# Layers 5 and 6, tokens, the state space and the gate scores of an audio tower, taken batch by batch into the groups of the convolution stream, whose loop is written out

## The chip, the cores and the metric

The kernel runs on 1 core of one Trainium2 chip. The metric is the device time of one execution, in microseconds (us). A core has five engines that each work through a queue of their own in program order: TensorE (PE in the rows; PEld is its weight load), VectorE (DVE), ScalarE (ACT), GpSimd (POOL) and SyncE (SP, which here only starts transfers). They wait for each other through semaphores. TensorE writes its products to PSUM, eight banks of 128 x 512 float32.

## The reference, cut to what matters

Eight rows of 120,000 samples pass seven strided convolutions, each followed by a layer norm over the 128 channels and a gelu. What comes out, 374 tokens of 128 channels per batch, is normed, projected to 192 features and taken through a diagonal state-space layer, a mixture of four experts, a two-way scan and a soft mixture of 64 experts.

```python
CONVS = [(128, 10, 5)] + [(128, 3, 2)] * 4 + [(128, 2, 2)] * 2
h = x[:, None, :]
for w, g, b, s in zip(conv_ws, ln_gs, ln_bs, strides):
    h = gelu(layernorm(conv1d(h, w, s)), exact)          # norm over the channels
h = layernorm(swapaxes(h, 1, 2)) @ proj_w + proj_b       # tokens
h = h + state_space(norm(h))   # x_s = A_bar x_(s-1) + B_bar u_s;  y_s = Re(C x_s) + D u_s
h = h + experts4(norm(h))      # scores = norm(h) @ gate_w + gate_b, argmax over 4
h = h + two_way_scan(norm(h))
h = h + soft_mixture(norm(h))  # 64 experts of 16 slots
```

## The kernel before

**setup** loads and centres the convolution weights. On DVE it also runs `ssm_tables` (L808 on, with helpers at L819 to L821), the decay and the tables of cosines and sines of the state space, for which ACT gives exponentials and sines in `ssm_functions` (L795 on). SP loads all small weights of later stages. A block of code ends when all engines have ended it.

**stream** computes layers 0 to 4 of all batches as one long sequence of 47 chunks (`CHUNKS`), in a hardware loop (`Fori`) on each engine. A chunk has eight groups (`GROUPS`), each the work of one half of a layer: on PE `conv(j, g)` makes 12 float32 products of 128x128 (6 for layer 4) at L255; ACT squares them (L312); DVE sums (`stats`, L352, and L355); POOL takes the power -0.5 (`root`, L426); DVE multiplies (`normalise`, L363); PE turns the result back to channels (`transposes`, L264), two groups late (`LAG = 2`); ACT applies the gelu (L330). Layer 0 of the next chunk, its patches and its windows are put between the groups: on PE behind groups 0 to 7 (L276, L286, L292, L302), on DVE in `copy_windows` (group 0), `patch_squares` and `patch_stats` (1), `copy_patches` (2, 3) and `split_patches` (6, 7), on POOL in `patch_root` (2 to 5). The order is written out by hand. Four PSUM banks take the products in turn (`BANKS = 4`). Behind the loop three last groups (`TAIL`) drain layers 3 and 4 one after the other. Layer 4 of all batches stays in the tile `l4`.

After the stream four stages each handle all eight batches before the next stage begins:

- **layers56** (L622 products, L641 squares, L659 and L663 sums, L675 roots, L654 multiplication, L614 turn, L634 gelu): layer 5 in 16 groups, layer 6 in 8, with a group's turn two groups late.
- **tokens**: turn, norm, turn back, affine, projection (L742), into the tile `h`.
- **state_space**: norm, turn, the products with B (L903, L904: 374 columns each), rotation by the tables (L969), two scans (L978, L979), rotation, the products with C (L916, L917), addition to `h` (L960). Batch b + 1 is prepared while b is computed; four banks take input products and turned tiles.
- **gate**: SP starts the loads of small tables, the clearing of a buffer of 2.6 MB in HBM (`sorted`), and the loads of the soft mixture's weights (`phA`, `phB`, `b2s`); DVE norms all 24 tiles; PE turns them and makes the scores (L1056 to L1067); DVE picks the expert and the row of each token. The block ends when the row numbers are there and SP has seen its loads land.

Behind it come `routed_ffn` and the later stages, the same in both kernels.

Of the kernel before, what the change touches and what calls it, by code (L numbers as in the profile page):

```python
# [12 lines left out]
P = 128  # L13
# [37 lines left out]
BANKS = 4  # L51
# [35 lines left out]

def setup(nc, T, S, io):

    with nc.Block() as block:  # L90
        @block.sync
        def _(sp):
# [11 lines left out]
            for name in ("proj_w", "BTa", "gate_wa", "Wia", "Wca", "Wcb", "Woa", "Wob", "lncol"):  # L104
                sp.dma_start(T[name][:], io[name]).then_inc(S["small_loaded"], 16)
            for name, rows in (("BTb", HIGH), ("gate_wb", HIGH), ("Wib", HIGH), ("Wcc", HIGH)):
                sp.dma_start(T[name][rows], io[name]).then_inc(S["small_loaded"], 16)
            sp.dma_start(T["mcol"][:, 0:15], io["mcol"]).then_inc(S["small_loaded"], 16)
            for name, n in (("rows", 3 * D), ("gate_row", 2 * N_EXPERT)):
                src = bass.AP(io[name].tensor, 0, [[0, TOK], [1, n]])  # L110
                sp.dma_start(view(T[name][:], [[1, n]]), src).then_inc(S["rows_loaded"], 16)
            sp.wait_ge(S["cols_loaded"], 16)
            sp.wait_ge(S["small_loaded"], 16 * 14)
            sp.wait_ge(S["rows_loaded"], 16 * 2)

        @block.gpsimd
        def _(pool):
# [8 lines left out]
            for name, rows in (("BTb", LOW), ("gate_wb", LOW), ("Wib", LOW), ("Wcc", LOW), ("phB", LOW)):  # L126
                pool.memset(T[name][rows], 0.0)
# [6 lines left out]
        def _(dve):  # L134
# [24 lines left out]
            dve.wait_ge(S["readout_loaded"], 16)  # L159
            ssm_tables(dve, T, S)  # L160

# [18 lines left out]
        @block.scalar  # L180
        def _(act):
            act.wait_ge(S["ident_ready"], 1)
            act.activation(T["identb"][:, :], T["ident"][:, :], ACT.Copy).then_inc(S["identb_ready"], 1)
            ssm_functions(act, T, S)
# [15 lines left out]
def stream(nc, T, S, io):  # L200
# [16 lines left out]
    def event(j, g):  # L217

        return GROUPS[g] + (g % BANKS, g % 2, count(j, g), P * j)

# [93 lines left out]
    def gelu(act, e, carry=None):  # L314
# [11 lines left out]
        if layer == 4:  # L326
            dst = T["l4"][:, :, bass.ds(column, P)]
# [106 lines left out]

    with nc.Block() as block:
        @block.sync
        def _(sp):
# [5 lines left out]
            with sp.Fori(0, CHUNKS) as j:  # L443
                load(j + 3)
            sp.wait_ge(S["x_loaded"], 16 * (CHUNKS + 3))

        @block.tensor
        def _(pe):
# [8 lines left out]
            with pe.Fori(0, CHUNKS) as j:  # L457
                for g in range(NG):
# [11 lines left out]
                    layer0s(pe, j + 1, L0_END.get(g, ()))  # L470
            transposes(pe, event(CHUNKS - 1, 6))
            transposes(pe, event(CHUNKS - 1, 7))
            for n, e in enumerate(TAIL):
                pe.wait_ge(S["h_ready"], END + n)
                products(pe, e)
                transposes(pe, e)

        @block.scalar
        def _(act):
            for i in range(8):  # L480
                gelu0(act, 0, i)
            with act.Fori(0, CHUNKS) as j:
                for g in range(NG):
# [8 lines left out]
                    for i in L0_END.get(g, ()):  # L492
                        gelu0(act, j + 1, i)
            gelu(act, event(CHUNKS - 1, 6))
            gelu(act, event(CHUNKS - 1, 7), CHUNKS + 1)
            for e in TAIL:
                square(act, e)
                gelu(act, e, CHUNKS + 1)

        @block.vector  # L500
        def _(dve):

            for name, n in (("normed", NG), ("turned", NG - LAG), ("h_ready", NG - LAG), ("summed", NG),
                            ("squared", NG), ("var_ready", NG), ("rstd_ready", NG), ("conv_done", NG), ("zz_done", 1)):
                dve.sem_inc(S[name], n)
            for c in range(2):
# [8 lines left out]
            with dve.Fori(0, CHUNKS) as j:  # L515
# [17 lines left out]
            for e in TAIL:  # L533
                stats(dve, e)
                normalise(dve, e)

        @block.gpsimd
        def _(pool):
# [3 lines left out]
            with pool.Fori(0, CHUNKS) as j:  # L542
# [4 lines left out]
            for e in TAIL:  # L547
                root(pool, e)

# [3 lines left out]


D = 192
D1, D2 = 128, D - 128
LOW, HIGH = slice(0, D2), slice(D2, P)
LEN = 374
TOK = 125
TPB = 3  # L560
SEQ = TOK * TPB
TILES = B * TPB
N_EXPERT, HID = 4, 768
HC = HID // P

ROUTED = (B * SEQ + N_EXPERT * (P - 1)) // P
SOFT_E, SLOT, SOFT_H = 64, 16, 384
SLOTS = SOFT_E * SLOT
SC = SLOTS // P
SHC = SOFT_H // P  # L570


class Link:


    def __init__(self, eng, sem, per_round=0, round_=0):
        self.eng, self.sem, self.base, self.n = eng, sem, round_ * per_round, 0

    def __call__(self, ins):
        self.n += 1  # L580
        ins.then_inc(self.sem, 1)
        self.eng.wait_ge(self.sem, self.base + self.n)


L4_FIRST = 513


def layers56(nc, T, S):

    psY, psT = T["psY"], T["psT"]

    def five(g, t, k):
        at = (L4_FIRST + k) // 2 + g * SEQ + t * TOK
        return T["l4"][:, (L4_FIRST + k) % 2, at:at + TOK]

    def six(g, t, k):  # L600
        at = 2 * (g * SEQ + t * TOK) + k
        return T["l5"][:, at:at + 2 * TOK - 1:2]

    def run(layer, groups, src, dst):
        s = {k: S[f"{k}{layer}"] for k in ("conv", "sq", "sum", "var", "rstd", "norm", "turn", "out")}
        with nc.Block() as block:
            @block.tensor
            def _(pe):
                def turn(g):
                    pe.wait_ge(s["norm"], g + 1)  # L610
                    if g >= 1:
                        pe.wait_ge(s["out"], g)
                    for t in range(TPB):
                        mm = pe.transpose(psT[:, t * TOK:(t + 1) * TOK], T["yn"][0:TOK, g % 2, t * C:(t + 1) * C],  # L614
                                          T["ident"][0:TOK, 0:TOK])
                    mm.then_inc(s["turn"], 1)
                for g in range(groups):
                    if g >= BANKS:
                        pe.wait_ge(s["norm"], g - BANKS + 1)
                    for t in range(TPB):  # L620
                        for k in range(2):
                            mm = pe.matmul(psY[g % BANKS][0:TOK, t * C:(t + 1) * C], src(g, t, k),  # L622
                                           T["wt"][:, 12 + 2 * (layer - 5) + k, :], start=(k == 0), stop=(k == 1))
                    mm.then_inc(s["conv"], 1)
                    if g >= LAG:
                        turn(g - LAG)
                for g in range(groups - LAG, groups):
                    turn(g)

            @block.scalar  # L630
            def _(act):
                def gelu(g):
                    act.wait_ge(s["turn"], g + 1)
                    act.activation(T[dst][:, g * SEQ:(g + 1) * SEQ], psT[:, 0:SEQ], ACT.Gelu,  # L634
                                   bias=T["cols"][:, 8 + layer:9 + layer],
                                   scale=T["cols"][:, layer:layer + 1]).then_inc(s["out"], 1)
                for g in range(groups):
                    act.wait_ge(s["conv"], g + 1)
                    if g >= 2:
                        act.wait_ge(s["sum"], g - 1)  # L640
                    act.activation(T["sq"][0:TOK, g % 2, 0:TPB * C], psY[g % BANKS][0:TOK, 0:TPB * C], ACT.Square)\  # L641
                        .then_inc(s["sq"], 1)
                    if g >= LAG:
                        gelu(g - LAG)
                for g in range(groups - LAG, groups):
                    gelu(g)

            @block.vector
            def _(dve):
                def normalise(g):  # L650
                    dve.wait_ge(s["rstd"], g + 1)
                    if g >= 2:
                        dve.wait_ge(s["turn"], g - 1)
                    dve.tensor_tensor(T["yn"][0:TOK, g % 2, 0:TPB * C].rearrange("p (t c) -> p t c", c=C),  # L654
                                      psY[g % BANKS][0:TOK, 0:TPB * C].rearrange("p (t c) -> p t c", c=C),
                                      bcast(T["rstd"][0:TOK, g % 2, 0:TPB], C), ALU.mult).then_inc(s["norm"], 1)
                for g in range(groups):
                    dve.wait_ge(s["sq"], g + 1)
                    dve.reduce_sum(T["ss"][0:TOK, g % 2, 0:TPB],  # L659
                                   T["sq"][0:TOK, g % 2, 0:TPB * C].rearrange("p (t c) -> p t c", c=C), axis=AX.X)\  # L660
                        .then_inc(s["sum"], 1)
                    dve.wait_ge(s["sum"], g + 1)
                    dve.tensor_scalar(T["var"][0:TOK, g % 2, 0:TPB], T["ss"][0:TOK, g % 2, 0:TPB], 1.0 / C, EPS,  # L663
                                      ALU.mult, ALU.add).then_inc(s["var"], 1)
                    if g >= 1:
                        normalise(g - 1)
                normalise(groups - 1)

            @block.gpsimd
# [1627 lines left out]
```

## Time and profile before

| | |
|---|---|
| median of 3 runs | 2589.71 us (2587.6 to 2591.08) |
| the profiled execution: time | 2585.41 us |
| the profiled execution: span | 2583.6 us |
| busy share of the span | PE 87%, DVE 54%, ACT 44%, POOL 34% |
| granted TensorE clock, mean | 0.933 of full speed |

The span is the time from the first to the last recorded instruction; 1.8 us lie around it. Shares are averages over stages with different limits, so they don't say what a change in one stage is worth. In the rows a clock of 1.00 is 2.4 GHz and 0.50 is 1.2 GHz.

### The profile page before, as it was taken

The numbers are of one execution on the slowest core, as the hardware profiler recorded it, in microseconds if no ns is written. First come the engines' busy times: TensorE is split into PE (matmuls) and PEld (weight loads), VectorE is DVE, ScalarE is ACT, GpSimd is POOL, SyncE is SP. The second block draws the span as 40 slices with busy tenths as digits, with TensorE's granted clock in tenths as the row PEclk, the third lists the DMA queues.
The fourth block names the chain that finished last, engine by engine and source line by source line (L and its number), as shares of the span: only waits on it lengthen the run. The fifth ranks groups of instructions, "written<-read, shape, count | busy, mean of one in ns | idle before, by whom it ended". The sixth has DMA issues, their size and how long they took to land. (4 is left out here: it accounts for less than half of the span.)

```text
span 2583.6 us, 48262 instructions
## 1 busy us (share of the span) xinstructions
PE 2236.5 (87%) x16651; PEld 2045.1 (79%) x16651; DVE 1394.8 (54%) x3521; ACT 1132.4 (44%) x2178; POOL 869.8 (34%) x758
## 2 busy tenths in 40 slices
PE   0999999999999999999987555199698788877988
PEld 0899999999999999999987434199455566667988
DVE  6566665666656666666654686212376465552222
ACT  0556656565565665656554100033233444432320
POOL 3545555454554545545443222500231000000000
PEclk9999999999999999999998776599899799988999
DMA  1000000000000000000000003578000011017976
GB/s 55 4 4 3 4 3 3 4 3 4 3 3 3 3 4 3 4 3 3 4 3 1 1 0 69 154 222 230 23 15 9 25 42 42 37 48 235 327 232 215
DMA packets 78675, 132.08 MB, mean 51 GB/s; under 512 B 13924, under 2 KB 56590, under 8 KB 77836
## 3 DMA queue, kind: packets, MB, share of 16 engines
q1 hardware_dynamic: 55052, 101.61, 12.6%
q10 hardware_dynamic: 17984, 20.30, 2.4%
q0 software_dynamic: 5568, 9.27, 1.2%
q8 instruction: 39, 0.64, 0.1%
q14 instruction: 32, 0.26, 0.0%
HBM read 102.57 MB, written 28.49 MB: 51 GB/s over the span
## 5 line engine op out<-in xcount | busy, mean ns | idle before, releaser
L255 PE MATMUL banks<-t_wt,t_l 128*128 128x128 f32 x8508 | 1043.0, 276 | 4.1 <-ACT t_l L330 2.9
L255 PEld LDWEIGHTS banks<-t_wt,t_l 128*128 128x128 f32 x8508 | 1012.5, 193 | 18.1 <-ACT t_l L330 3.9
L426 POOL TENSOR_TENSOR t_rstd<-t_var,t_minus_half 128x4 f32<-128x4 f32 (+1 forms) x379 | 366.8, 968 | 626.4 <-DVE t_var L355 626.4
L363 DVE TENSOR_TENSOR t_yn<-banks,t_rstd 128x512 f32<-128x512 f32 (+1 forms) x379 | 249.2, 657 | 344.9 <-POOL t_rstd L426 326.5
L312 ACT ACTIVATE t_sq<-banks 128x512 f32<-128x512 f32 (+1 forms) x379 | 215.9, 570 | 480.2 <-PE banks L255 477.9
L432 POOL TENSOR_TENSOR t_zrstd<-t_zvar,t_minus_half 128x8 f32<-128x8 f32 x196 | 320.8, 1638 | 43.2 <-DVE t_zvar L390 43.2
L343 ACT ACTIVATE t_l<-banks,t_cols 128x512 f32<-128x512 f32 x384 | 292.7, 778 | 47.6 <-PE banks L302 41.9
L352 DVE TENSOR_REDUCE t_ss<-t_sq 128x4 f32<-128x512 f32 (+1 forms) x379 | 244.5, 645 | 110.9 <-ACT t_sq L312 110.9
L330 ACT ACTIVATE t_l<-banks,t_cols 128x512 f32<-128x512 f32 (+2 forms) x381 | 285.1, 748 | 10.7 <-PE banks L264 5.9
L264 PE MATMUL banks<-t_ident,t_yn 128*128 128x128 f32 x1426 | 219.4, 273 | 11.5 <-DVE t_yn L363 10.3
L264 PEld LDWEIGHTS banks<-t_ident,t_yn 128*128 128x128 f32 x1426 | 173.5, 141 | 25.4 <-DVE t_yn L363 11.3
L697 POOL TENSOR_TENSOR t_nrstd<-t_nvar,t_minus_half 125x3 f32<-125x3 f32 x40 | 34.5, 861 | 394.4 <-DVE t_nvar L691 394.4
L302 PE MATMUL banks<-t_p60T,t_w 120*128 120x512 bf16 x384 | 140.3, 386 | 1.1 <-ACT t_l L343 1.0
L1277 ACT ACTIVATE t_G<-banks,t_b1T 128x128 f32<-128x128 f32 x162 | 47.9, 365 | 87.1 <-PE banks L1244 87.0
L1673 ACT ACTIVATE t_EDT<-banks,t_ltm 128x374 f32<-128x374 f32 x64 | 36.8, 575 | 111.3 <-DVE t_ltm L1779 111.0
L1916 DVE TENSOR_SCALAR t_a<-t_H,t_egA 128x128 f32 x64 | 22.1, 346 | 115.3 <-PE banks L1849 107.6
L1848 PE MATMUL banks<-t_a,t_w 128*128 128x128 f32 x384 | 75.8, 279 | 5.6 <-DMA t_w1x<-in_w1x 5.6
L1979 PE MATMUL banks<-t_yb,t_ectb 128*125 128x192 f32 (+1 forms) x384 | 65.6, 333 | 14.4 <-DVE t_yb L1954 10.4
L1979 PEld LDWEIGHTS banks<-t_yb,t_ectb 128*125 128x125 f32 (+1 forms) x384 | 64.0, 192 | 16.0 <-DVE t_yb L1954 10.7
L1779 DVE TENSOR_REDUCE t_ltm<-banks 128x1 f32<-128x374 f32 x64 | 34.8, 544 | 75.8 <-PE banks L1563 75.8
L1849 PE MATMUL banks<-t_a,t_w1x 65*128 65x128 f32 x384 | 75.7, 279 | 0.0
L1856 PE MATMUL banks<-t_w,t_eg 128*128 128x192 f32 x384 | 73.6, 328 | 0.7 <-ACT t_eg L1875 0.6
(311 smaller groups left out, 3428.0 us busy)
## 6 DMA issues: line engine op xcount, KB each, us to landing
t_w<-in_w SPq DMA_DIRECT2D x64, 480.0 KB
t_w<-in_w SPq DMA_DIRECT2D x27, 576.0 KB, 6.5
ect<-t_ECT SPq DMA_DIRECT2D x16, 750.0 KB, 3.2
t_w1a<-in_w1a SPq DMA_DIRECT2D x27, 384.0 KB, 3.8
t_ectb<-ect ACTq DMA_DIRECT2D x5, 1500.0 KB, 7.9
t_w1x<-in_w1x SPq DMA_DIRECT2D x64, 97.5 KB
ys<-t_ye ACTq DMA_DIRECT2D x64, 96.0 KB
t_yb<-ys ACTq DMA_DIRECT2D x8, 768.0 KB, 11.0
```

Of the source, the lines that this page charges most:

```text
L255: mm = pe.matmul(psY[bank][:, t * C:(t + 1) * C], src[:, at:at + P], T["wt"][:, 3 * (layer - 1) + k, :], start=(k == 0), stop=(k == 2))
L264: mm = pe.transpose(psT[:, t * P:(t + 1) * P], T["yn"][:, par, t * C:(t + 1) * C], T["ident"][:, :])
L302: pe.matmul(psL[i % 2][:, :], T["w60"][:, slot, :], p60T[:, 4 * q:4 * q + 4, :].rearrange("r a p -> r (a p)"), start=True, stop=True).then ...
L312: act.activation(T["sq"][:, par, 0:n], psY[bank][:, 0:n], ACT.Square).then_inc(S["squared"], 1)
L330: act.activation(dst, psT[:, 0:n].rearrange("c (t p) -> c t p", p=P), ACT.Gelu, bias=T["cols"][:, 8 + layer:9 + layer], scale=T["cols"][:, ...
L343: act.activation(view(T["l0"][:, :], [[2 * BLOCK, 4], [1, P]], block_at(0, 8 * q + slot)), psL[i % 2][:, :].rearrange("c (a p) -> c a p", ...
L352: dve.reduce_sum(T["ss"][:, par, 0:n], T["sq"][:, par, 0:n * C].rearrange("p (t c) -> p t c", c=C), axis=AX.X)\
L363: dve.tensor_tensor(T["yn"][:, par, 0:n * C].rearrange("p (t c) -> p t c", c=C), psY[bank][:, 0:n * C].rearrange("p (t c) -> p t c", c=C), ...
L426: pool.tensor_tensor(T["rstd"][:, par, 0:n], T["var"][:, par, 0:n], T["minus_half"][:, 0:n], ALU.pow)\
L432: pool.tensor_tensor(T["zrstd"][:, s], T["zvar"][:, s], T["minus_half"][:, 0:POS // 4], ALU.pow)\
L1848: pe.matmul(o, T["w12"][:, r, c * P:(c + 1) * P], T["a1"][:, r % RING, :], start=True, stop=False)
L1979: mm = pe.matmul(pO[k % 2][0:n, 0:D], T["ectb"][:, b % MIX_RING, c, t * TOK:t * TOK + n], T["yb"][:, b % MIX_RING, c, :], start=(c == 0), ...
```

## The change

The stages layers56, tokens, state_space and the scores half of gate are gone. Their work is cut into 33 steps per batch (`CHAIN = 33`), and one step is put behind each group of the stream, on each engine's queue, once the batch's part of `l4` is there: batch b has the steps 0 to 32 behind the groups of chunk 8 + 6b and on. Batches 0 to 5 fit whole; of batch 6 the last three chunks take steps 0 to 23, the three groups of `TAIL` steps 24 to 26, and steps 27 to 32 and all 33 of batch 7 come behind `TAIL`. All steps share one bank, `psQ`, so each waits for the one before. The stream has `BANKS = 3`. `ssm_tables` becomes a generator whose 40 pieces are put behind DVE's first 40 groups, `ssm_function` stands at three places of ACT's stream, and SP's small loads move from setup behind the second load of the stream. The loops on all five engines are written out. `phA`, `phB` and `b2s` now share memory with the steps' tiles and are still loaded in gate.

```diff
-BANKS = 4
+BANKS = 3
...
+    def chain_at(j, g):
+
+        if j < FIRST_OF:
+            return 0, -1
+        return (j - FIRST_OF) // PERIOD, NG * ((j - FIRST_OF) % PERIOD) + g
...
+    def pe_conv56(pe, b, i):
+        e = 3 * b + i
+        if i == 0:
+            pe.wait_ge(S["h_ready"], last_column_of(b))
+            if b >= 1:
+                pe.wait_ge(S["z_read"], b)
+        else:
+            pe.wait_ge(S["q_out"], e)
+        for t in range(TPB):
+            for k in range(2):
+                src = five(b, i, t, k) if i < 2 else six(t, k)
+                mm = pe.matmul(psQ[0:TOK, t * C:(t + 1) * C], src, T["wt"][:, 12 + 2 * (i // 2) + k, :],
+                               start=(k == 0), stop=(k == 1))
+        mm.then_inc(S["q_conv"], 1)
+
+    def pe_turn56(pe, b, i):
+        pe.wait_ge(S["q_norm"], 3 * b + i + 1)
...
+    def pe_turn_u(pe, b, part):
+        if part == 0:
+            pe.wait_ge(S["u_ready"], b + 1)
...
+    def pe_state_outputs(pe, b, part):
+        if part == 0:
+            pe.wait_ge(S["x_ready"], b + 1)
...
+    def pe_chain(pe, b, step):
...
+        if step == 0:
+            pe_conv56(pe, b, 0)
+        if step == 2:
+            pe_turn56(pe, b, 0)
+        if step == 3:
+            pe_conv56(pe, b, 1)
+        if step == 5:
+            pe_turn56(pe, b, 1)
+        if step == 6:
+            pe_conv56(pe, b, 2)
+        if step == 8:
+            pe_turn56(pe, b, 2)
+        if step == 9:
+            pe_tokens(pe, b)
+        if step == 11:
+            pe_channels(pe, b)
+        if step == 12:
+            pe_project(pe, b, 0)
+        if step == 13:
+            pe_project(pe, b, 1)
+        if step == 16:
+            pe_turn_u(pe, b, 0)
+        if step == 17:
+            pe_turn_u(pe, b, 1)
+        if step == 18:
+            pe_state_inputs(pe, b, 0)
+        if step == 19:
+            pe_state_inputs(pe, b, 1)
+        if step == 26:
+            pe_state_outputs(pe, b, 0)
+        if step == 27:
+            pe_state_outputs(pe, b, 1)
+        if step == 30:
+            pe_turn_v(pe, b, 0)
+        if step == 31:
+            pe_turn_v(pe, b, 1)
+        if step == 32:
+            pe_scores(pe, b)
...
+    def dve_chain(dve, b, step):
+        if step == 0:
+            dve_stats56(dve, b, 0)
+        if step == 1:
+            dve_normalise56(dve, b, 0)
...
+        if step == 9:
+            dve_token_stats(dve, b)
+        if step == 10:
+            dve_token_norm(dve, b)
...
+        if step == 14:
+            dve_u_stats(dve, b)
+        if step == 15:
+            dve_u(dve, b)
+        if step == 18:
+            dve_rotate_inputs(dve, b, 0)
+        if step == 19:
+            dve_rotate_inputs(dve, b, 1)
+        if step == 20:
+            dve_join_inputs(dve, b)
+        if step == 21:
+            dve_scan(dve, 0)
+        if step == 22:
+            dve_scan(dve, 1)
+        if step == 23:
+            dve_rotate_states(dve, b, 0)
+        if step == 24:
+            dve_rotate_states(dve, b, 1)
+        if step == 25:
+            dve_rotate_states(dve, b, 2)
...
+        if step == 28:
+            dve_v_stats(dve, b)
+        if step == 29:
+            dve_v(dve, b)
...
-            with pe.Fori(0, CHUNKS) as j:
+            for j in range(CHUNKS):
                 for g in range(NG):
                     conv(pe, j, g)
...
                     layer0s(pe, j + 1, L0_END.get(g, ()))
+                    pe_chain(pe, *chain_at(j, g))
             transposes(pe, event(CHUNKS - 1, 6))
             transposes(pe, event(CHUNKS - 1, 7))
             for n, e in enumerate(TAIL):
                 pe.wait_ge(S["h_ready"], END + n)
                 products(pe, e)
                 transposes(pe, e)
+                pe_chain(pe, B - 2, LEFT + n)
+            for step in range(LEFT + len(TAIL), CHAIN):
+                pe_chain(pe, B - 2, step)
+            for step in range(CHAIN):
+                pe_chain(pe, B - 1, step)
...
                     if g == 7:
                         split_patches(dve, j + 2, 1)
+                    next(tables, None)
+                    dve_chain(dve, *chain_at(j, g))
...
         @block.gpsimd
         def _(pool):
+            pool.memset(T["phB"][LOW], 0.0)
             pool.memset(T["w1b"][LOW, :, :], 0.0).then_inc(S["zero_ready"], 1)
```

## Rows read from the trace of the kernel before

**Rows 1.** Busy time by stage: one stream chunk, TAIL, layers56, tokens, state_space, gate.
```profile
core 0: us, PE busy (x) PEld busy (x) DVE busy (x) ACT busy (x) POOL busy (x), PEclk, DMA share, GB/s
1179.30:1206.10 26.80, 26.80 (x242) 26.27 (x241) 16.47 (x38) 16.16 (x29) 14.10 (x13) 1.00 0.01 3
1337.00:1368.00 31.00, 14.62 (x67) 12.06 (x65) 7.21 (x20) 6.47 (x13) 3.41 (x4) 0.66 0.01 3
1368.00:1423.00 55.00, 46.94 (x358) 43.91 (x359) 28.72 (x72) 25.98 (x47) 20.41 (x24) 0.91 0.00 1
1423.00:1461.00 38.00, 23.19 (x99) 17.92 (x99) 23.54 (x104) 5.97 (x9) 6.80 (x8) 0.76 0.00 1
1461.00:1585.40 124.40, 71.04 (x208) 47.23 (x208) 104.65 (x217) 6.86 (x16) 29.24 (x24) 0.71 0.00 0
1585.40:1636.60 51.20, 31.00 (x148) 30.31 (x148) 23.22 (x111) 8.43 (x18) 10.20 (x9) 0.50 0.40 87
```

**Rows 2.** Timeline of setup: start, duration, engine, line, operation [idle before it].
```profile
17.18 0.16 DVE L823 TENSOR_TENSOR t_sv<-t_sv 128x1 f32<-128x1 f32 x1
17.28 12.16 SPq L102 DMA_DIRECT2D t_band<-t_gram  x16
...
17.60 1.28 ACT L804 ACT_TABLE_LOAD   x1
...
42.91 2.29 DVE L163 TENSOR_REDUCE t_wmean<-t_wt 128x16 f32<-128x2048 f32 x1
...
48.21 0.70 PE L286 MATMUL banks<-t_ident,t_xs 128*85 128x128 f32 x2 [31.15 <-PEq L90]
```

**Rows 3.** PE by line: the stream chunk of Rows 1, then one line of the whole run.
```profile
L255 PE MATMUL banks<-t_wt,t_l 128*128 128x128 f32 x180 | 21.9, 275 | 0.0
...
L1352 PE MATMUL banks<-t_xA,t_Wca 128*128 128x374 f32 x144 | 49.2, 477 | 0.0
```

**Rows 4.** Timeline of one stream chunk around the groups 0, 7 and again 0.
```profile
1181.93 0.67 DVE L352 TENSOR_REDUCE t_ss<-t_sq 128x4 f32<-128x512 f32 x1
...
1184.09 0.69 DVE L363 TENSOR_TENSOR t_yn<-banks,t_rstd 128x512 f32<-128x512 f32 x1 [1.29 <-POOL t_rstd L426]
...
1185.69 0.60 PE L264 MATMUL banks<-t_ident,t_yn 128*128 128x128 f32 x4
...
1206.18 2.84 PE L255 MATMUL banks<-t_wt,t_l 128*128 128x128 f32 x24
...
1207.58 0.23 DVE L416 COPY t_p<-t_p 128x320 bf16<-128x320 bf16 x1
```

**Rows 5.** Operations of the stages that move, by line, whole run: busy us, mean ns.
```profile
L697 POOL TENSOR_TENSOR t_nrstd<-t_nvar,t_minus_half 125x3 f32<-125x3 f32 x40 | 34.5, 861 | 394.4 <-DVE t_nvar L691 394.4
...
L969 DVE TENSOR_TENSOR t_seq<-t_seq 128x374 f32<-128x374 f32 x32 | 17.9, 560 | 1.8
...
L978 DVE TENSOR_TENSOR_SCAN t_seq<-t_sv,t_seq 128x374 f32<-128x374 f32 x8 | 7.5, 937 | 0.3
```

**Rows 6.** Timeline: the last group of TAIL, its products and its gelu.
```profile
1359.99 2.93 PE L255 MATMUL banks<-t_wt,t_l 128*128 128x128 f32 x12 [1.10 <-ACT t_l L330]
...
1366.02 0.56 ACT L330 ACTIVATE t_l<-banks,t_cols 128x256 f32<-128x256 f32 x1 [2.67 <-PE banks L264]
```

**Rows 7.** PE's timeline between layer 5 and layer 6, and the clock there.
```profile
1402.92 6.95 PE L622 MATMUL banks<-t_wt,t_l 128*125 128x128 f32 x36 [1.01 <-PEq L606]
...
1404.00:1406.00 2.00, 2.00 (x11) 2.00 (x11) 0.00 (x0) 0.14 (x1) 0.00 (x0) 0.50 0.02 4
```

**Rows 8.** Gate: its first memset, and the DMA share where its loads end.
```profile
1585.44 3.93 POOL L1038 MEMSET t_w1b<- 64x4608 f32 x1 [21.15 <-POOLq L891]
...
1608.00:1610.00 2.00, 2.00 (x11) 2.00 (x11) 0.00 (x0) 0.00 (x0) 0.00 (x0) 0.50 0.33 41
1610.00:1612.00 2.00, 2.00 (x12) 2.00 (x11) 0.00 (x0) 0.86 (x2) 0.00 (x0) 0.50 0.00 0
```

**Rows 9.** The page's DMA queues that bring instructions: packets, MB, share of 16 engines.
```profile
q8 instruction: 39, 0.64, 0.1%
```

More of the change, by code:

```diff
@@ L326, in gelu @@
         if layer == 4:
[L327 removed]
+            dst = T["l4"][:, :, column:column + P]
         else:
@@ new lines, in last_column_of, with five, six @@
+    def last_column_of(b):
+        return END + 3 if b == B - 1 else count(FIRST_OF - 1 + PERIOD * b, 4)
+    def five(b, half, t, k):
+        at = (L4_FIRST + k) // 2 + (2 * b + half) * SEQ + t * TOK
+        return T["l4"][:, (L4_FIRST + k) % 2, at:at + TOK]
+    def six(t, k):
+        return T["l6_in"][:, 2 * t * TOK + k:2 * (t + 1) * TOK + k - 1:2]
+    def pe_conv56(pe, b, i):
[12 more added lines that the diff above has]
+        mm.then_inc(S["q_conv"], 1)
@@ new lines, in pe_channels, with pe_project @@
+    def pe_channels(pe, b):
+        pe.wait_ge(S["tok_normed"], b + 1)
+        for t in range(TPB):
+            mm = pe.transpose(psQ[:, t * TOK:(t + 1) * TOK], T["nTok"][0:TOK, t * C:(t + 1) * C], T["ident"][0:TOK, 0:TOK])
+        mm.then_inc(S["tok_back"], 1)
+    def pe_project(pe, b, part):
+        if part == 0:
+            pe.wait_ge(S["tok_affine"], b + 1)
+        else:
+            pe.wait_ge(S["tok_out"], 2 * b + 1)
+        for t in ((0, 1), (2,))[part]:
+            mm = pe.matmul(psQ[0:TOK, t % 2 * D:(t % 2 + 1) * D], T["nCh"][:, t * TOK:(t + 1) * TOK], T["proj_w"][:, :],
+                           start=True, stop=True)
+        mm.then_inc(S["tok_projected"], 1)
@@ L456, in _ @@
             layer0s(pe, 0, range(8))
-            with pe.Fori(0, CHUNKS) as j:
+            for j in range(CHUNKS):
                 for g in range(NG):
@@ L481, in _ @@
                 gelu0(act, 0, i)
-            with act.Fori(0, CHUNKS) as j:
+            for j in range(CHUNKS):
                 for g in range(NG):
@@ L505, in _ @@
                 dve.sem_inc(S[name], n)
+            tables = ssm_tables(dve, T, S)
+            chain_link.eng = dve
             for c in range(2):
@@ L514, in _ @@
                 split_patches(dve, c, 1)
-            with dve.Fori(0, CHUNKS) as j:
+            for j in range(CHUNKS):
                 for g in range(NG):
@@ L541, in _ @@
                     patch_root(pool, c, part)
-            with pool.Fori(0, CHUNKS) as j:
+            for j in range(CHUNKS):
                 for g in range(NG):
@@ L570 @@
[L570 to L669, printed above, removed]
-            def _(pool):
-                for g in range(groups):
-                    pool.wait_ge(s["var"], g + 1)
-                    if g >= 2:
-                        pool.wait_ge(s["norm"], g - 1)
-                    pool.tensor_tensor(T["rstd"][0:TOK, g % 2, 0:TPB], T["var"][0:TOK, g % 2, 0:TPB],
-                                       T["minus_half"][0:TOK, 0:TPB], ALU.pow).then_inc(s["rstd"], 1)
-    run(5, 2 * B, five, "l5")
-    run(6, B, six, "l6")
@@ L683, in norm_stats @@
+                pool_chain(pool, B - 2, LEFT + n)
+            for step in range(LEFT + len(TAIL), CHAIN):
+                pool_chain(pool, B - 2, step)
+            for step in range(CHAIN):
+                pool_chain(pool, B - 1, step)
 def norm_stats(dve, T, S, link, k, get, width):
```

728 lines of the change are left out of this document (401 added, 327 removed).

## The prediction, as put on record

> **What bounds the kernel now.** I read the busy time by stage first [rows 1]. In a stream chunk PE is busy for all of its 26.8 us, at full clock, while DVE, ACT and POOL are busy for 16.5, 16.2 and 14.1 us. 47 such chunks are 1260 us, so about 49% of the span is PE-bound without a gap. Then come 31 us of TAIL (PE 14.6 busy), 55 us of layers56, 38 of tokens, 124 of state_space (PE 71, DVE 105 busy) and 51 of gate: latency and DVE, with TensorE at 0.5 to 0.9 of its clock. The reader is to see two things: the moved stages hold no engine fully, and the place they move to has no free PE time.
>
> The timeline of a chunk [rows 4] shows how far DVE is behind PE. For group 0 the sum starts at 1181.93, the multiplication ends at 1184.78, and PE turns the result at 1185.69: 0.9 us of slack. From the start of a sum to the end of the multiplication pass 2.7 to 2.85 us, over half of it waiting for POOL, and in this order nothing else of DVE's can stand between but the copies that are there. So DVE's own loop is not its 16.5 busy us: seven groups of 2.7, one of 2.1 for two tiles, and 3.9 us outside them (windows, patch sums, two splits) are 24.9 of the 26.8 us. DVE is second in line by 2 us a chunk.
>
> **What is removed.** (a) The three stages: TAIL ends at 1366.6, layers56 starts at 1368.0, gate at 1585.4 [rows 1, 6]: 217.5 us. (b) In gate DVE's norms and the scores go, but SP's loads stay, in the same order, and the block waits for them. They began with the block at 1585.4 and DMA falls silent by 1610 [rows 8]; one memset now stands ahead of them (1 us). The rest of gate took 51.2 us; it will take 25, not the 10 that its DVE work takes: -26. (c) Setup: `ssm_tables` held DVE from 17.2 to 42.9, while SP's 16 band transfers were issued by 29.4, and PE's stream started at 48.2 [rows 2]. Without the tables the bands decide, and PE starts at about 31.4 (29.4, and a landing between 0 and 3 us, of which I take 2): -17. Sum: -260.5.
>
> **What is added.** (d) The tables, 25.7 us, now lie in 40 pieces of 0.64 us on DVE in five chunks: 24.9 + 5.1 is 3.2 over 26.8, less 0.5 a chunk for the loop's branch, less 2 us of slack once: +12. ACT changes its table six times, 1.28 us each [rows 2], and has 10 us free in a chunk: +3. The bounds are 0 and 26. The Trainium skill (ScalarE: Activation LUTs, "What ACT_TABLE_LOAD costs") counts 2.66 us per change with the drain; by it the six would be 16 us of ACT instead of 8, and the term 3 to 8.
>
> (e) PE's own work. 242 records in 26.8 us are 0.111 us each; a 374-column record takes 49.2/144 = 0.34 [rows 1, 3], a 192-column one by length 0.17. Per batch: layers 5 and 6 36 records, scores 12, turns 27 (together 75, 8.4 us); projection 6 and outputs 12 of 192 columns, 3.1; inputs 8 of 374, 2.7: 14.2 us. Nothing covers it, since PE has no gap. Six batches and 10.2 us for steps 0 to 23 of batch 6: +95.
>
> (f) Waits of PE inside the chain. PE comes to step k + 1 at a fixed time, DVE to step k only after its multiplication of group k. In the chunk as it is, DVE's free point against PE's next step is: group 7, 1.9 us late (its copies end at 1207.8 to 1208.0, PE's step would stand at 1206.1) [rows 4]; group 0 1.8, group 1 1.5, group 2 0.0, groups 4 and 5 early by 0.9 and 0.4. To this come DVE's step and what it did for the chain just before. I passed once through the 33 steps, PE's point and DVE's point group by group, with a 374-column operation at 0.56, a scan at 0.94 and POOL's root at 0.86 [rows 5]. PE waits: at step 2 for `normalise56`, 1.7; at step 8 2.1; at 11 0.5; at 16 for u, whose statistics and application (1.4 and 1.0) stand behind both splits, 4.6; behind step 24, where the copied windows are late after scan and rotation, 1.5; at 26 for the rotated states, 4.2; at 30 0.6. Sum 15.3 per batch, each wait delaying everything behind it, since all engines are in order. Six batches and the first four waits of batch 6, 8.9: +101. Behind a PE wait also stand the stream's own products, so ACT and DVE wait too and cannot make up for it; POOL's `root` of the next group waits behind `root56` but is early by over 1 us. Bounds: DVE's excess alone (its loop and 23 us of steps against PE's lengthened groups) gives 5 per batch, 35; the waits without any recovery between them give 19 per batch, 125. I take the pass, as each of its terms has a row.
>
> BANKS = 3 costs nothing: a group's products wait for the multiplication of three groups before, which PE has already waited for in its turn two groups late. It costs only if `LAG` grew.
>
> (g) What stands bare at the end. TAIL stays, +1 for DVE's later start. Batch 6 has steps 26 to 32 left: outputs and adds 5.6, norm, turns and scores 9: 14.5. Batch 7 has all 33 in a row, nothing beside them. The last group of TAIL, the same chain of engines with 12 records, took 6.6 us from products to gelu at two tiles [rows 6]; three tiles make 7.5, three groups 22.4. Three norms at 3.4 (10), six turns at low clock with five copies (8.5), projection (3.7), scores (2.7): 25. State space: inputs 2 x 4 x 0.68 at half clock, 13 DVE operations 8.5, outputs 12 x 0.34, adds: 19.5. Sum 67, between 55 (full clock) and 75. Altogether +83.
>
> (h) The clock. Between layer 5 and layer 6 PE did 1 us of work in 4.6 us; the 36 records from 1402.92 on took 6.95 us, against 4.0 at 0.111, at a clock of 0.50 [rows 7]: 2.9 us lost. Thirteen waits in the stream are over 4 us. Bounds 0 and 38; I take 9, because the chunks ahead of such a wait are full and the row's were not. The Trainium skill (TensorE: Matmul & The Clock Gate, "Loop structure matters more than you think") calls long waits between matmuls bad for the clock and a vector-engine copy harmless; by it the term is 38 if these count as long, 0 if they count as copies.
>
> Sum: -260.5 + 15 + 95 + 101 + 83 + 9 = +42.5 us. Made against the span of 2583.6: 2626; with the 1.8 us around it 2628, which as a change of the median (2589.7, 4.3 above the profiled execution) is 2632 us, 1.6% slower.
>
> **Rivals.** *A, DVE keeps up (faster).* Place: the waits of (f). The sum turns at waits of 8.9 us per batch (42.5 less over 6.6 batches). For it: by busy time DVE has 10 us free in a chunk and the chain brings 23 per six; 15 of 48 groups are free of steps. Against it: 24.9 of 26.8, above. At DVE's excess alone (5 per batch, clock untouched) the time is 2632 - 66 - 9 = 2557. Chance 0.25. *B, the turning point:* waits of 8 to 10 per batch, 2590 within 0.2%, about what a measurement of this kernel can tell from no change: 0.05. *C, the forecast,* waits of 10 to 19: 2595 to 2665, 0.55. *D, instructions.* The written-out stream has to be fetched; the larger queue of instructions brought 0.64 MB in the whole run [rows 9], and 47 chunks of code replace one. Straight code ran in layers56 at 6.5 PE records a us, the stream runs at 9.0 [rows 1]. If a fetch held PE once per chunk for 1 us: 47 more, 2679. Also here: the clock falls at every long wait (+29). Chance 0.15. That the steps don't run in the stream at all is excluded by the queues' order.
>
> **Range and chances.** 2557 to 2680: it leaves out 0.10 below and 0.10 above. C's own range is 2595 to 2665. Slower 0.70, same 0.05, faster 0.25.
>
> **What would show it.** PE's stream starts at 31 to 32 us. Chain-free chunks keep 26.8 us; the six chunks of a batch take 190 instead of 161, with PE waiting for `u` (step 16) and the states (step 26) for over 4 us each. The stream with TAIL ends near 1565, batch 7 takes 67 us behind it with TensorE at 0.5, and gate lasts 25 us, held by SP. I am wrong if the batch period is under 184, if batch 7 takes under 50, or if chain-free chunks are longer than 27.5 (fetching).

## The result and the profile after

The changed kernel takes 2605.48 us (median of 4 runs, 2604.19 to 2609.97) against 2588.65 for the kernel before beside it: ratio 1.0066, 95% interval 1.0053 to 1.0079. It is slower, by 17 us, where I had forecast 42.5. Its profiled span is 2604.7 us, 21.1 more than before's; the sums below are made against that. A chunk is counted from PE's transposes of the windows (L305), which stand behind its group 0.

Busy time of the kernel after by stretch (columns as in [rows 1]): the stream's start up to the mark of chunk 0, the six chunks with the tables, two without a step, batches 0 to 5, batch 6's three chunks, TAIL, batch 6's rest, batch 7, gate.

```profile
29.80:62.10 32.30, 17.00 (x64) 11.48 (x65) 9.73 (x26) 7.50 (x11) 12.91 (x8) 1.00 0.19 59
62.10:234.00 171.90, 164.16 (x1443) 157.83 (x1442) 116.75 (x330) 105.85 (x180) 84.80 (x72) 1.00 0.02 6
234.00:287.60 53.60, 53.60 (x482) 52.53 (x481) 32.71 (x76) 32.28 (x57) 28.19 (x25) 1.00 0.02 5
287.60:1423.70 1136.10, 1073.82 (x9248) 1039.05 (x9247) 705.08 (x1729) 613.26 (x1075) 555.54 (x481) 0.98 0.02 4
1423.70:1520.00 96.30, 90.36 (x765) 86.77 (x763) 59.38 (x148) 51.68 (x91) 48.49 (x43) 0.96 0.01 3
1520.00:1549.10 29.10, 13.78 (x64) 11.59 (x63) 10.88 (x26) 5.73 (x12) 3.40 (x4) 0.65 0.01 3
1549.10:1563.10 14.00, 8.08 (x32) 6.18 (x32) 3.46 (x14) 1.53 (x3) 0.85 (x1) 0.54 0.00 1
1563.10:1629.80 66.70, 31.75 (x101) 22.27 (x101) 20.61 (x60) 6.06 (x11) 7.89 (x8) 0.55 0.00 0
1629.80:1655.70 25.90, 1.13 (x4) 0.92 (x4) 8.74 (x35) 1.57 (x2) 6.18 (x7) 0.50 0.74 172
```

Two chunks without a step take 53.6 us with PE busy throughout, 26.8 each as in [rows 1]: written-out code costs nothing there. Six chunks with a batch's steps take 189.4 us (1136.1 / 6) against 161.0. Batch 7 takes 66.7 us with PE busy for 31.7 at a clock of 0.55. PE's waits in batch 1's six chunks (line, releaser: us in all, times, longest):

```profile
PE banks L532 <- DVE t_u L697: 4.0, 1, 4.0
PE banks L551 <- DVE t_late L756: 2.3, 1, 2.3
PE banks L500 <- DVE t_yn L682: 1.9, 2, 1.5
PE banks L311 <- DVE t_xT L395: 0.9, 1, 0.9
PE banks L295 <- DVE t_zz L401: 0.9, 1, 0.9
PE banks L562 <- DVE t_v L697: 0.3, 1, 0.3
```

That is 10.3 us in 28.4. All are for DVE: the turn of `u` (step 16), the state outputs (step 26), the turns of layers 5 and 6 (steps 2 and 8), and two of the stream's own, the windows and the patches, behind the scans. The longest in batch 0, on PE's timeline and then on DVE's:

```profile
347.17 2.84 PE L274 MATMUL banks<-t_wt,t_l 128*128 128x128 f32 x24
...
354.57 0.54 PE L532 MATMUL banks<-t_ident,t_u 125*128 125x125 f32 x3 [3.91 <-DVE t_u L697]
354.95 4.47 PE L274 MATMUL banks<-t_wt,t_l 128*128 128x128 f32 x24
```

```profile
348.25 0.33 DVE L429 CAST t_p<-t_rest 128x320 bf16<-128x320 f32 x1
348.49 0.87 DVE L688 BATCH_NORM_STATS2 t_cbn<-t_h 125x6 f32<-125x192 f32 x3
...
349.82 0.68 DVE L371 TENSOR_REDUCE t_ss<-t_sq 128x4 f32<-128x512 f32 x1
...
351.85 0.69 DVE L382 TENSOR_TENSOR t_yn<-banks,t_rstd 128x512 f32<-128x512 f32 x1 [1.15 <-POOL t_rstd L445]
352.46 0.48 DVE L432 TENSOR_TENSOR t_p<-t_rest,t_p 128x320 bf16<-128x320 f32 x1
...
353.56 0.96 DVE L697 TENSOR_SCALAR t_u<-t_h,t_cmv,t_crstd 125x192 f32<-125x192 f32 x3 [0.16 <-DVE t_p L435]
```

The first split ends at 348.6, the statistics of `u` behind it delay the sum of group 7 to 349.82, its multiplication comes at 351.85, the second split stands next, and only then `u`. Behind the wait the 24 products take 4.47 us in place of 2.84; the granted clock of two stretches there (duration, busy times, PEclk as in [rows 1]):

```profile
353.00:357.00 4.00, 2.43 (x16) 2.43 (x17) 2.68 (x10) 0.48 (x1) 1.28 (x2) 0.84 0.02 4
357.00:361.00 4.00, 4.00 (x28) 4.00 (x27) 1.33 (x4) 1.50 (x4) 1.10 (x1) 0.74 0.00 0
```

So behind a wait of 3.9 us TensorE ran part of both stretches at the lower level, 1.2 GHz; the products of the group after that took 2.85 us again. Gate ends on SP's loads, as [rows 8] had it; DVE's last result and what it does next:

```profile
1644.26 0.18 DVE L1292 CAST t_row<-t_top 125x24 int32<-125x24 f32 x1
...
1645.03 3.90 SPq L1217 DMA_DIRECT2D t_late<-in_soft_b  x8
1655.68 1.22 DVE L1428 TENSOR_TENSOR t_phq<-t_late 128x1024 f32<-128x1024 f32 x1 [11.25 <-PEq L1196]
```

The queue of instructions ([rows 9]) brought more than three times as much, in a stream whose chunks are no longer for it:

```profile
q8 instruction: 128, 2.10, 0.3%
```

### The profile page after: what moved, and what is told of

Its sections match the earlier page's. It is cut to its first block and busy times, and to the rows that moved or that the text cites. A ratio compares the mean times of both kernels' runs of the same rounds, so it can differ in the third digit from the quotient of the medians.

```text
span 2604.7 us, 45184 instructions
## 1 busy us (share of the span) xinstructions
PE 2231.2 (86%) x16651; PEld 2040.5 (78%) x16651; DVE 1372.6 (53%) x3533; ACT 1135.7 (44%) x2183; POOL 870.8 (33%) x763
## 5 line engine op out<-in xcount | busy, mean ns | idle before, releaser
L274 PE MATMUL banks<-t_wt,t_l 128*128 128x128 f32 x8508 | 1060.9, 279 | 4.1 <-ACT t_l L349 2.9
L274 PEld LDWEIGHTS banks<-t_wt,t_l 128*128 128x128 f32 x8508 | 1031.3, 196 | 17.8 <-ACT t_l L349 4.1
L349 ACT ACTIVATE t_l<-banks,t_cols 128x512 f32<-128x512 f32 (+1 forms) x381 | 284.7, 747 | 11.0 <-PE banks L283 6.2
L1058 POOL TENSOR_TENSOR t_nrstd<-t_nvar,t_minus_half 125x3 f32<-125x3 f32 x24 | 20.7, 863 | 289.2 <-DVE t_nvar L1052 289.2
L2047 DVE TENSOR_SCALAR t_a<-t_H,t_late 128x128 f32 (+1 forms) x128 | 38.1, 339 | 116.3 <-PE banks L1980 108.2
L1804 ACT ACTIVATE t_EDT<-banks,t_ltm 128x374 f32<-128x374 f32 x64 | 36.8, 574 | 111.3 <-DVE t_ltm L1910 111.0
```

Source lines behind the costliest of these rows:

```text
L274: mm = pe.matmul(psY[bank][:, t * C:(t + 1) * C], src[:, at:at + P], T["wt"][:, 3 * (layer - 1) + k, :], start=(k == 0), stop=(k == 2))
L349: act.activation(dst, psT[:, 0:n].rearrange("c (t p) -> c t p", p=P), ACT.Gelu, bias=T["cols"][:, 8 + layer:9 + layer], scale=T["cols"][:, ...
```

## The experiments

Ratios are to the kernel before, run beside each; the changed kernel has 1.0066, and 0.001 is 2.6 us.

**e1: the tables back in setup.** Undoes terms (c) and (d).

```diff
 setup, DVE:   +for _ in ssm_tables(dve, T, S): pass
 setup, ACT:   +for n in range(3): ssm_function(act, T, S, n)
 stream, DVE:  -next(tables, None)
```

> The changed kernel with one part undone: the tables of the state space and their three ACT functions are computed in setup again, where the kernel before had them, and nothing of them in the stream; the chain stays. By the reading of the two traces (setup without the tables starts PE 18.4 us earlier, the pieces in the stream cost 10.9 us over six chunks) this is 7.5 us slower than the changed kernel, 2612 to 2614, with all chain-free chunks at 26.8. If the pieces were not what lengthened those six chunks, they stay at 28.4 and it is 18 us slower, 2623. If the setup's gain was not from the tables, it is faster than the changed kernel by 11, 2594.

1.0089 (1.0073 to 1.0106). This is 6 us above the changed kernel, where I had expected 7.5. In its trace PE's stream starts 17.0 us later than in the changed kernel's (46.84 and 29.82) and chunk 0 is 16.3 later. Every chunk before the steps takes 26.84 (six of them took 27.8 to 29.2), 10.9 less in all, so the steps begin 5.4 us later. Both terms are what they were read as, within 1.4 us.

**e4: the kernel before, loops written out, three banks.**

```diff
-BANKS = 4
+BANKS = 3
-with pe.Fori(0, CHUNKS) as j:        (on all five engines)
+for j in range(CHUNKS):
```

> The kernel before with two parts of the change alone: the stream's loop of 47 chunks written out on every engine, and three banks of products in place of four (the bank of a group then depends on the chunk, so the loop can't stay). No step is moved. Theory: both cost nothing, since PE is busy through each chunk with or without the loop; the time is within 3 us of the kernel before, 2586 to 2592. Rival, code that is fetched: 0.5 to 1 us a chunk, 2612 to 2636. Rival, banks: products wait for the multiplication three groups back, and a chunk takes over 27.5 us.

0.9993 (0.9983 to 1.0003), no difference. Its chunks take 26.83, with the same 128 packets of instructions. The fetching of rival D and a price of the fourth bank are refuted; the other half of D, the clock, comes up in e6.

**e3: the same steps, three groups later; e9: spread evenly; e2: spread by hand.** Each changes only which step of batches 0 to 5 stands behind which of the 48 groups.

```diff
-return (j - FIRST_OF) // PERIOD, NG * ((j - FIRST_OF) % PERIOD) + g
+b, slot = (j - FIRST_OF) // PERIOD, NG * ((j - FIRST_OF) % PERIOD) + g
+return b, (slot if b == B - 2 else STEP_IN[slot])      # STEP_IN inverts SLOT_OF
 e3: SLOT_OF[k] = k + 3
 e9: SLOT_OF[k] = k * 47 // 32
 e2: SLOT_OF = [0, 1, 3, 4, 5, 7, 8, 9, 11, 12, 13, 15, 16, 17, 19, 21, 23,
                24, 26, 27, 28, 29, 34, 35, 36, 37, 39, 40, 42, 43, 45, 46, 47]
```

> The changed kernel with the steps of batches 0 to 5 as dense as they are, but begun three groups later in the chunk. Theory: what a step waits depends on the group beside which DVE's part of it stands; step 15 (u) moves from group 7 to group 2 and the scans from groups 5 and 6 to 0 and 1. PE's wait for u, 4.0 us, falls to about 2, with it the low clock behind it (2 us), the waits behind the scans (0.9, 0.9 and 2.3) fall to about 3 in all, and another of 1 to 2 us may come where steps 3 to 5 meet groups 6 and 7: 3 to 5 us per batch gained, 18 to 30 in all, about 2580. Rival, the waits are the chain's own latency and stand wherever it begins: the same within 5 us, 2605.

> The changed kernel with the 33 steps of batches 0 to 5 spread evenly over their 48 groups (about two groups with a step, one without), without regard to which step waits or to what DVE does in a group. It tells pacing from placing. If free groups alone are what counts, the period is that of the paced kernel, 178 us, and the time 2538. If the place counts, waits of 2 us stay at one to three steps per batch whose DVE part stands beside groups 6, 7 or 0: a period of 180 to 183 us, 2550 to 2570. I expect 2552.

> The changed kernel with the 33 steps of batches 0 to 5 spread over their 48 groups by hand: an empty group before each step at which PE waits for DVE, DVE's longer steps in groups 1 to 5 and none of them in groups 6 and 7, where DVE splits the patches. Batches 6 and 7 as they are. Theory: PE waits because DVE has one group less than it needs between two steps, not because DVE lacks time over the six chunks. Then the 10.3 us of waits per batch and the 2 to 4 us at low clock behind them go, the batch's six chunks fall from 189.4 to 176 to 178 us (161 and 15 us of PE's own work), and the time is 68 to 80 us lower, about 2532. Rival 1, DVE has no time over: its excess moves from the chain's waits to the stream's, the period stays over 187 and the time is 2590 to 2605. Rival 2, only half goes, because the steps' own work on DVE makes the next multiplication late wherever it stands: 2565.

The ratio of e3 is 1.0013 (1.0000 to 1.0025), that of e9 0.9868 (0.9853 to 0.9883) and that of e2 0.9797 (0.9781 to 0.9814). The rows show one batch in each, in the same order:

```profile
475.76:662.58 186.82, 178.41 (x1543) 171.92 (x1542) 118.47 (x288) 102.30 (x180) 92.64 (x81) 0.99 0.02 4
```

```profile
469.05:650.29 181.24, 176.19 (x1544) 170.48 (x1542) 118.12 (x290) 102.50 (x180) 92.66 (x80) 1.00 0.02 4
```

```profile
464.55:642.75 178.20, 175.45 (x1543) 170.50 (x1542) 117.88 (x290) 102.09 (x180) 92.63 (x80) 1.00 0.02 4
```

DVE does the same 118 us of work in all; what differs is PE's idle time and its clock. In e3 the wait for `u` fell from 4.0 to 0.3 us, more than its theory says (to 2), and others came up: 2.7 at the turn of `v`, 1.9 at the state outputs, 1.6 at a turn of layers 5 and 6. The six periods are 186.8 to 188.8 us, on average 1.7 below the changed kernel's, and the time fell by 14 us where I had expected 18 to 30. Even pacing takes 8 us off the period, as expected; its longest wait, 2.2 us, is again the one for `u`. Pacing by hand takes 11 us off it, 70 us in all, which is at the near end of the 68 to 80 expected. In e2 2.7 us of waits are left in a batch:

```profile
PE banks L554 <- DVE t_h L768: 1.8, 1, 1.8
PE banks L524 <- DVE t_h L717: 0.5, 1, 0.5
PE banks L496 <- DVE t_z L785: 0.4, 1, 0.4
```

The period of 178.2 less these is 175.5, PE's busy time there: 161.0 and 14.5 of the chain's.

**e11: DVE's step ahead of the splits, otherwise dense.**

```diff
+dve_chain(dve, *chain_at(j, g))
 if g == 6: split_patches(dve, j + 2, 0)
 if g == 7: split_patches(dve, j + 2, 1)
-dve_chain(dve, *chain_at(j, g))
```

> The changed kernel, dense as it is, with DVE's step of the chain ahead of the patch splits in groups 6 and 7 and not behind them; no other engine's order changes. Theory, from the trace of the changed kernel: the second split (1.1 us) stands between group 7's multiplication and the application of u, and in the same way ahead of step 7's multiplication. Both waits of PE shrink by 1.1 us, from 4.0 to 2.9 and from 1.5 to 0.4, and if 2.9 us no longer bring the clock down, 2 us more per batch are gained: 2.2 to 4.2 us in seven batches, 15 to 28 us less than the changed kernel, about 2583. Rival: the split is needed as early as the step (the patch transposes of the next chunk wait for it, or the windows' copy), and what is gained at one wait is lost at another: 2605.

1.0000 (0.9991 to 1.0010), 17 us less than the changed kernel for one line moved on one engine. DVE's timeline where `u` is made in batch 1:

```profile
535.43 0.69 DVE L382 TENSOR_TENSOR t_yn<-banks,t_rstd 128x512 f32<-128x512 f32 x1 [1.12 <-POOL t_rstd L445]
536.04 0.95 DVE L697 TENSOR_SCALAR t_u<-t_h,t_cmv,t_crstd 125x192 f32<-125x192 f32 x3
536.90 0.49 DVE L432 TENSOR_TENSOR t_p<-t_rest,t_p 128x320 bf16<-128x320 f32 x1
```

PE's waits fell to 2.3 to 2.5 us at `u` and 0.3 at step 8. The clock still fell behind the former in batches 1 to 4 and 6 (in batch 5 behind 2.2 us of waiting for the samples just ahead), so the low clock's part of the gain stayed away (in batches 1 to 4 the chunk with `u` took 34.1 to 34.4 us, in batch 0 32.7). Here are the four us behind the wait in batch 1, then in batch 0, where the clock stayed up:

```profile
537.00:541.00 4.00, 3.96 (x21) 3.96 (x22) 2.69 (x8) 0.48 (x1) 1.70 (x2) 0.57 0.00 0
```

```profile
351.20:355.20 4.00, 3.99 (x35) 3.99 (x36) 2.69 (x9) 1.18 (x4) 1.73 (x2) 1.00 0.02 4
```

**e6: PE kept busy in its waits.** Extra transposes of the identity that nobody reads.

```diff
+FILL = {2: 22, 5: 22, 8: 22, 11: 26, 16: 30, 26: 56, 30: 30}       # batch 7, ahead of these steps
+FILL_IN_STREAM = {16: ("tok_out", 30), 26: ("ssm_in", 16)}         # batches 0 to 5; 16 in batch 6 too
+for _ in range(n):
+    pe.transpose(bank[:, 0:P], T["ident"][:, :], T["ident"][:, :])
```

> The changed kernel with extra transposes of the identity, whose results nobody reads, where PE waits: 30 before the turn of u and 16 before the state outputs in the stream, and 22 to 56 ahead of each of the seven longer waits of batch 7. The chain's waits stay. Theory: behind the 4.0 us waits for u PE ran 3 to 4 us at the lower clock (24 products took 4.5 to 4.9 us in place of 2.84), 19 us in the whole stream; with PE busy the clock stays at 1.00 there and the stream is 12 to 19 us shorter. In batch 7 PE's own work of 31.7 us at a clock of 0.5 falls to about 18 and batch 7 from 66.6 to about 55, if the extra work brings the clock up. Together about 2580. Rival: the clock does not rise in batch 7, the extra transposes take twice their time and end after DVE is done, and batch 7 takes 70 to 80 us: 2600 to 2610. Second rival: the lower clock in the stream comes from DVE's or ACT's part and stays, and nothing is gained there.

0.9960 (0.9946 to 0.9974), 27 us less than the changed kernel. PE around the turn of `u` in batch 1, then batch 7:

```profile
536.31 3.44 PE L578 MATMUL banks<-t_ident 128*128 128x128 f32 x30
540.49 0.54 PE L532 MATMUL banks<-t_ident,t_u 125*128 125x125 f32 x3 [0.73 <-DVE t_u L710]
540.86 2.85 PE L274 MATMUL banks<-t_wt,t_l 128*128 128x128 f32 x24
```

```profile
1545.10:1599.60 54.50, 42.62 (x309) 36.98 (x309) 20.62 (x60) 6.05 (x11) 7.91 (x8) 0.97 0.00 1
```

DVE is as late as before, but the 24 products behind take 2.85 us again. The chunk with `u` takes 34.1 to 34.2 us in every batch; in the changed kernel it took 35.8 to 36.8. The next chunk, with the state outputs, takes 34.7 to 35.0 us, and had taken 34.7 in three batches and 36.3 to 36.7 in the other three. So the low clock had cost 17 us in six batches and 2 in batch 6. Batch 7 takes 54.5 us in place of 66.7 with three times as many records. Both rivals fall. The Trainium skill (TensorE: Matmul & The Clock Gate, "Loop structure matters more than you think") calls long waits between matmuls bad for the clock; the trace agrees at 3.9 to 4.0 us, and at 2.3 to 2.5 us in most batches of e11, so here waits for vector work count among them.

**e5: gate's largest load issued early; e8: the tables beside groups 1 to 5 only.**

```diff
 e5, SP at the start of the stream (and no longer in gate):
+src = bass.AP(T["h"][:, :, :].tensor, (TILES - 1) * D, [[TILES * D, P], [0, ROUTED], [1, D]])
+sp.dma_start(io["sorted"].rearrange("(n p) d -> p n d", p=P), src).then_inc(S["early_clear"], 16)
 e8, DVE in the stream:
-next(tables, None)
+if 1 <= g <= 5: next(tables, None)
```

> The changed kernel with one DMA moved: the clearing of the routed buffer in DRAM (2592 KB, the largest of gate's loads) is issued at the start of the stream, from a part of h that is still zero, and gate no longer has it. Theory, as in the forecast: gate's 24.3 us are held by SP's loads, since DVE has its last result (the rows) at 1644.4 and the block ends at 1655.6. Without the clearing DVE's chain decides, gate takes 13 us, and the whole is 11 us faster than the changed kernel, about 2594. Rival, another of the loads (the eight of soft_b2, which come last, or their issuing) holds the block just as long: within 3 us of the changed kernel, 2605.

> The changed kernel with one line more: the 40 pieces of the tables stand only beside groups 1 to 5 of the first eight chunks, none beside groups 6, 7 and 0, where DVE splits the patches and copies the windows. Theory: the 10.9 us that the table chunks cost are DVE being late there by 0.64 us a group, with no group to catch up in. Spread so, a chunk has three groups to catch up in, and the cost falls to 0 to 3 us: 8 to 11 us less than the changed kernel, about 2596. Rival: the pieces cost what they are wherever they stand (DVE's chunk is full): the eight chunks together are again 11 us longer, 2605.

The ratio of e5 is 1.0045 (1.0028 to 1.0062), 5 us less where 11 were expected. Gate itself is 7.6 us shorter (24.3 to 16.7); where the other 2 us went isn't shown. DVE now goes on 3.7 us behind its last result, and not 11.25:

```profile
1647.80 1.23 DVE L1429 TENSOR_TENSOR t_phq<-t_late 128x1024 f32<-128x1024 f32 x1 [3.70 <-PEq L1201]
```

The clearing did hold gate. For these 3.7 us the other loads still do, for DMA is busy up to 1646.0; that the last eight, of `soft_b2`, are what counts is likely from their place and not tested. The ratio of e8 is 1.0030 (1.0018 to 1.0042), 9 us less: its first eight chunks take 216.6 us, 1.9 over the 214.7 of the kernel before, and the chunk behind them 0.8 more than in the changed kernel. The tables' price was their place, and what ACT's changes of table cost there is within those 1.9 us.

**e7, e10, e12: put together.** e7 is e2 with batch 6's steps 24 to 31 on both sides of TAIL's transposes; e10 adds e5, e8 and the extra transposes in batch 7, in TAIL and at batch 6's turn of `u`; e12 adds e11's order.

```diff
+IN_TAIL = [((24, 25), (26,)), ((27, 28), (29,)), ((30,), (31,))]    # ahead of, behind transposes
+AFTER_TAIL = (32,)
```

> The paced kernel with batch 6's last steps put closer into the three groups of TAIL: steps 24 to 31 before and behind TAIL's transposes, where PE waits for DVE and ACT (14 of 29 us busy), and only step 32 left behind it. Theory: TAIL's waits of 2.4 to 3.4 us are latency of its own chain and take the steps in; of the 14 us of batch 6's rest 9 to 12 go, TAIL grows by 2 to 4: 6 to 10 us less than the paced kernel, about 2530. Rival: each step put in makes TAIL's next multiplication late by as much, and nothing is gained: 2538.

> The paced kernel with batch 6's end inside TAIL, the clearing issued early, the tables' pieces beside groups 1 to 5, and extra transposes of the identity where PE waits in batch 7, in TAIL and before the turn of u in batch 6. If the gains add up: 2530.5 for the paced kernel with TAIL filled, less 11 for batch 7, 5 to 8 for the clearing, 8 to 10 for the tables, 2 to 5 for TAIL and batch 6's clock: 2498, that is 3.5% below the kernel before. If the extra transposes in TAIL come on top of its chain, 2505.

> The kernel of e10 with the same order on DVE. There the steps of batches 0 to 5 that stand beside groups 6 and 7 need no DVE, so only batch 6, which is dense, can gain: 1 to 3 us, 2492 to 2495. Rival: the windows' copy of the next group comes later and costs a microsecond or two somewhere in 47 chunks, 2497.

The ratio of e7 is 0.9770 (0.9754 to 0.9786), 7 us below e2. That of e10 is 0.9634 (0.9621 to 0.9647), 2495.2 us where 2498 were expected; the gains add up. Batch 7 there, at full clock throughout:

```profile
1468.90:1521.80 52.90, 40.90 (x309) 35.26 (x309) 20.46 (x59) 6.05 (x11) 7.91 (x8) 1.00 0.00 1
```

The ratio of e12 is 0.9584 (0.9571 to 0.9597), 2483.6 us, 4.2% below the kernel before and 8 us better than I said. I had overlooked that `SLOT_OF` puts steps 26 and 32, which have a part on DVE, beside group 7, in e2 already. PE's wait behind step 26 fell from 1.8 to 0.6, the one of 0.4 behind step 32 is gone, and a batch takes 176.4 us.

## Why the prediction was right or wrong

The direction was right, and the size too large: 2.5 times by the medians (42.5 and 17 us), twice by the profiled spans (42.5 and 21.1). By its own steps, in the profiled span:

| step | forecast | measured |
|---|---|---|
| (a) stages removed | -217.5 | -217.5 |
| (b) gate, 51.3 to 24.3 | -26 | -27 |
| (c) setup, mark of chunk 0 at 62.1, not 79.0 | -17 | -16.8 |
| (d) tables in the stream | +15 | +10.9 |
| (e) PE's own work of the steps | +95 | +102 |
| (f) PE's waits in the chain | +101 | +68 |
| (g) TAIL +1.0, batch 6's rest 14.0, batch 7 66.7 | +83 | +82 |
| (h) low clock in the stream | +9 | +19 |
| behind gate | 0 | +2 |
| sum; seams between stages -1.5 | +42.5 | +21.1 |

The measured waits are six batches at 10.3 us and 5.9 in batch 6. The low clock is taken from e6. Term (e) is the rest of what the stream grew by behind chunk 8 (188.7 us), so it holds what restarts cost behind each wait; e2's busy time gives 14.5 per batch against my 14.2.

**The step that failed is (f), in its size.** The mechanism stood: PE waits for DVE's steps, longest for `u`, whose statistics and application stand behind the splits (moving DVE's step ahead of them in e11 took some 1.6 us off that wait), then for the states. But the pass by hand gave 15.3 us per batch (its terms add up to 15.2), and 10.3 came: 0.4 where I had 1.7 (step 2), 1.5 for 2.1 (8), 0 for 0.5 (11), 4.0 for 4.6 (16), 1.8 for 1.5 (behind 24), 2.3 for 4.2 (26), 0.3 for 0.6 (30). Six of the seven were too long.

Two reasons can be read. The first is that I took DVE's free points from the loop. There DVE stands idle for 0.61 us at each chunk's start, ahead of the copy of the windows. Here are PE's mark of a chunk and this copy in the kernel before (the multiplication of group 0 behind them is at 1184.09 in [rows 4]):

```profile
1179.13 0.38 PE L286 MATMUL banks<-t_ident,t_xs 128*85 128x128 f32 x2
...
1181.59 0.42 DVE L376 COPY t_xT<-banks 85x256 f32<-85x256 f32 x1 [0.61 <-DVE t_p L416]
```

In e4, the same work written out, 0.14 us of the gap are left:

```profile
1180.46 0.38 PE L286 MATMUL banks<-t_ident,t_xs 128*85 128x128 f32 x2
...
1181.98 0.24 DVE L416 COPY t_p<-t_p 128x320 bf16<-128x320 bf16 x1
1182.36 0.42 DVE L376 COPY t_xT<-banks 85x256 f32<-85x256 f32 x1
...
1184.70 0.69 DVE L363 TENSOR_TENSOR t_yn<-banks,t_rstd 128x512 f32<-128x512 f32 x1 [1.12 <-POOL t_rstd L426]
```

From the mark to the multiplication of group 0 pass 4.96 us in the loop and 4.24 written out. I had allowed for the branch in (d), but the 1.8 and 1.5 us by which DVE is late at groups 0 and 1 in (f) hold it: they should have been 1.1 and 0.8. That is 0.7 of the 1.3 us too much at step 2, and it can be as much at step 26, whose states are rotated beside groups 7, 0 and 1. The second reason is smaller: I charged 0.56 for each 374-column operation, its duration, while in the trace the next one starts 0.46 us after it where it waits for nothing. There are 12 of them in a batch. Behind those of the inputs DVE stood idle anyway, so only the six that rotate the states count, four of them with such a start: 0.4 us. Some 3 to 4 of the 4.9 us are left for which I can name no cause, and neither reason had a run of its own.

**(h) was half of what came.** I took 9 us "because the chunks ahead of such a wait are full". Fullness ahead did not help: the clock fell behind the waits for `u` in all seven batches, and behind the 2.3 us waits for the states in three of six.

**(c), (b) and (g) held** within 1.3 us each, batch 7 within 0.3, but (c) by two errors that cancel. PE's stream started at 29.8, 1.6 us earlier than my 31.4, and the first group's 24 products took 5.46 us where they had taken 4.31. That gate is held by SP is shown by e5, though the clearing alone decides only part of it. (d) was 4 too high.

**The signs.** I had said that six chunks of a batch would take 190 us, and they took 189.4, but this is luck in part: by my own terms it should have been 192, and 5 us less of waiting were met by more for the clock and the restarts. The wait for the states was to be over 4 us and was 2.3. The stream with TAIL was to end near 1565 and ended at 1549, so most of what I was off by lies there. In the reading of [rows 4], DVE waits for POOL for 1.1 to 1.3 us of 2.7 to 2.85, which is under half and not over; no term rests on it.

**The rivals.** A, that DVE keeps up, was wrong for this order, and right that DVE has the time: by hand the same steps take 2538 us, and spread evenly 2557.6. That this is the value I gave A is no confirmation, since A was about the dense order, though the waits in e9 are the 5 us per batch that A had. In the dense order DVE's free time stands in the 15 groups behind the chain. So slower was the result of the order, not of moving the work. The fetching of D is refuted by e4 and the chunks of 26.8 us. Its other half, that the clock falls at every long wait, came true in part: it fell ten times in the batches' chunks and cost 19 us, where D had 38.

## What to carry to other kernels

When steps of a long dependent chain are put behind the groups of a full engine's loop, spread them over all the groups there are, and keep the second engine's part away from the groups where its own copies stand: here that was worth 2.7% of the time, four times what the change itself had cost. Look at which operations stand between a multiplication and a step in the second engine's queue before moving anything else; one line reordered gave 17 us. Take the second engine's free points from code in the form in which it will run: a loop's gap at its start is gone when the loop is written out. And an idle stretch of TensorE of 4 us, here often one of 2.3, has a second price behind it, which work that nobody reads saved.

## What the runs showed of the hardware

The clock has a price behind a wait: behind 3.9 to 4.0 us of idle time the next 24 products took 4.47 to 5.10 us in place of 2.84, in each of seven batches, although PE had been busy for 29 us ahead of it with no gap over 0.15 us. Behind 2.3 us the clock fell in some batches and not in others, in the same code. With 208 extra transposes in PE's waits the 33 steps of batch 7 ran at 0.97 for 54.5 us (e6) and at 1.00 for 52.9 (e10), where without them they had 0.55 over 66.7. A loop's turn left DVE idle for 0.61 us, where the written-out code has 0.14. Two MB of instructions for the written-out code, three times as much as before, delayed nothing that the chunks show.
